# Another layout for the split keys in device memory, and shorter value visits, in a gated cross-attention block with experts

## The reference, cut to what matters

```
q, k, v = LN(x) @ W_Q, ctx @ W_K, ctx @ W_V       # 16 heads of 8 columns
score = where(mask == 0, -1e9, q k^T / sqrt(8))   # [4, 16, 256, 1601]
attn  = softmax(score) @ v
x  = x + tanh(g_xattn) * (attn @ W_T)
h  = LN(x);  probs = softmax(h @ router_w.T);  top 2 of 8 experts
x  = x + tanh(g_ffn) * sum_e combine_e * ((silu(h w1a_e) * (h w1b_e)) @ w2_e)
```

## Time and profile before

| | |
|---|---|
| Median of 3 runs (lowest to highest) | 483.82 us (476.94 to 484.28) |
| The profiled execution's own time | 477.56 us |
| Its span, first to last instruction | 475.8 us |
| Busy: PE, DVE, ACT, POOL | 93%, 74%, 57%, 18% |
| Mean granted TensorE clock | 0.975 of full speed |
| The chain that ended last: PE, DVE, ACT, DMA | 72%, 13%, 5%, 3% |
| First scores on PE | at 43.7 us |
| DMA traffic | 35.2 MB, mean 74 GB/s |

### The profile page before, as it was taken

The page is one execution under the profiler, slowest core; times in us unless marked ns, Lnnn a source line. Parts: engine busy times, 40 slices in busy tenths (PEclk is TensorE's granted clock), DMA queues, the critical chain, the costliest instruction groups (busy, mean ns, idle before and its releaser), DMA issues.

```text
span 475.8 us, 10097 instructions
## 1 busy us (share of the span) xinstructions
PE 442.1 (93%) x3864; PEld 268.5 (56%) x3866; DVE 350.7 (74%) x768; ACT 273.4 (57%) x569; POOL 86.2 (18%) x207
## 2 busy tenths in 40 slices
PE   7883999998999999999999999999999999999596
PEld 3331455654555556666655566666645476766495
DVE  3971787675668898887888987888879888542386
ACT  4201566674768666665667665665667666677131
POOL 4800507337820100000001000000001000000000
PEclk9986999999999999999999999999999999999599
DMA  7377537593735040404014403012061200000000
GB/s 272 96 162 170 124 106 160 160 269 107 187 114 104 2 91 0 92 3 91 3 28 87 94 0 80 13 43 51 2 114 43 50 2 1 2 2 24 0 1 11
DMA packets 20701, 35.23 MB, mean 74 GB/s; under 512 B 2236, under 2 KB 12924, under 8 KB 20524
## 3 DMA queue, kind: packets, MB, share of 16 engines
q1 hardware_dynamic: 19348, 33.96, 29.8%
q10 hardware_dynamic: 1304, 0.59, 0.5%
HBM read 26.49 MB, written 7.80 MB: 72 GB/s over the span
## 4 chain that ended last, share of the span: by engine, by line
PE 72%; DVE 13%; ACT 5%; issue 4%; DMA 3%; POOL 2%; POOLq 0%; SPq 0%; DVEq 0%; ACTq 0%
PE banks L1049 20%; PE banks L1015 17%; PE banks L997 13%; PE banks L1073 10%; PE banks L1081 5%; DVE chunk_max L751 4%; DVE chunk_max L733 3%; ACT probs L626 3%; PE banks L904 2%; PE banks L898 2%; DMA queries<-neg_rows 2%; DVE late L835 1%; DMA probs<-x 1%; PE banks L1131 1%; DVE late L839 1%
## 5 line engine op out<-in xcount | busy, mean ns | idle before, releaser
L751 DVE TENSOR_REDUCE chunk_max<-banks 128x1 f32<-128x512 f32 (+1 forms) x390 | 240.0, 663 | 63.4 <-PE banks L997 62.6
L626 ACT ACTIVATE probs<-banks 128x512 f32<-128x512 f32 x384 | 210.7, 603 | 88.9 <-PE banks L1015 88.3
L1015 PE MATMUL banks<-queries,keys 75*128 75x256 bf16 (+1 forms) x832 | 156.9, 275 | 10.2 <-DMA queries<-neg_rows 7.2
L997 PE MATMUL banks<-keys,queries 72*128 72x512 bf16 x480 | 146.0, 338 | 2.0 <-ACT probs L626 0.7
L1015 PEld LDWEIGHTS banks<-queries,keys 75*128 75x128 bf16 (+1 forms) x832 | 72.6, 100 | 77.6 <-DVE chunk_max L751 26.7
L1049 PE MATMUL banks<-probs,value_t 128*9 128x256 f32 x1536 | 91.9, 380 | 0.0
L1073 PE MATMUL banks<-late,w 128*128 128x256 f32 x256 | 67.2, 392 | 0.0
L1049 PEld LDWEIGHTS banks<-probs,value_t 128*9 128x9 f32 x1536 | 37.4, 90 | 43.7 <-issue 10.3
L997 PEld LDWEIGHTS banks<-keys,queries 72*128 72x128 bf16 x480 | 42.3, 97 | 21.6 <-ACT probs L626 7.6
L1073 PEld LDWEIGHTS banks<-late,w 128*128 128x128 f32 x256 | 47.9, 196 | 8.3 <-issue 2.6
L649 ACT ACTIVATE late<-banks 128x256 f32<-128x256 f32 x64 | 24.6, 385 | 45.7 <-PE banks L1073 38.8
(11 more groups left out here) (116 smaller groups left out, 261.9 us busy)
## 6 DMA issues: line engine op xcount, KB each, us to landing
keys<-k_parts SPq DMA_DIRECT2D x48, 300.2 KB
k_parts<-split SPq DMA_DIRECT2D x6, 400.2 KB, 7.6
ctx_in<-ctxT SPq DMA_DIRECT2D x3, 800.5 KB, 5.6
k_parts<-late SPq DMA_DIRECT2D x6, 400.2 KB, 4.9
queries<-q_parts SPq DMA_DIRECT2D x16, 144.0 KB
w<-w1T SPq DMA_DIRECT2D x1, 2048.0 KB, 12.7
q_parts<-q_split SPq DMA_DIRECT2D x9, 192.0 KB, 2.6
w<-mask SPq DMA_DIRECT2D x2, 800.5 KB, 7.0
```

Of the source, the lines that this page charges most:

```text
L626: nc.scalar.activation(probs[:, s % (HELD * QH), :], ring[ring_bank["scores", n]][:, :], ACT.Exp, scale=SCALE).then_inc(probs_ready, 1)
L751: nc.vector.reduce_max(dst, src, axis=AX.X).then_inc(chunk_used, 1)
L997: last = nc.tensor.matmul(dst[:, i * CW[c]:(i + 1) * CW[c]], queries[q][0:ROWS, j, t * P:(t + 1) * P], keys[q][0:ROWS, j, c * BANK:c * BAN ...
L1015: last = nc.tensor.matmul(dst, keys[q][0:KR, j, t * P:t * P + w], queries[q][0:KR, j, :], start=True, stop=not with_mask)
```

## The change

- `k_parts` becomes [batch, part, q, column, head of the unit, 1632]: for one part, one q and one column, the four heads of a unit lie side by side, and each row is padded from 1601 to 1632 columns. `split0`, `split1` and `keys` get the same padded width.
- A key load still has three transfers to 24 partitions each, but each partition's four rows of 3202 bytes become one row of 13,056 bytes. The source is now given as part by column ([3, 8] rows), where it was one run of 24 rows by 4 heads.
- A store still has 128 source partitions, but its target is given as [4 heads, 32 rows, 1632], where it was [16 heads, 8 rows, 1601].
- GpSimd clears the padding of `split0` and `split1` once each; SP waits for the first of these before it copies the rows of ones.
- Values: in units 4, 8 and 12 the tiles come two at a time.

```diff
-        k_parts_dram = nc.dram_tensor("k_parts", [B, H, PARTS, DH, SK], BF16).ap()
+        k_parts_dram = nc.dram_tensor("k_parts", [B, PARTS, NQ, DH, QH, SKP], BF16).ap()
...
-        split0 = sb("split0", [P, PARTS, SK], BF16)
+        split0 = sb("split0", [P, PARTS, SKP], BF16)
...
-        keys = [sb(f"keys{i}", [P, QH, SK], BF16) for i in range(NQ)]
+        keys = [sb(f"keys{i}", [P, QH, SKP], BF16) for i in range(NQ)]
...
                 for c in range(PARTS):
                     rows = slice(c * PARTS * DH, (c + 1) * PARTS * DH)
-                    sp.dma_start(keys[q][rows, :, :],
-                                 k_parts_dram[b, q::NQ].rearrange("j p d k -> (p d) j k")).then_inc(ld_unit[q], 16)
+                    sp.dma_start(keys[q][rows, :, :].rearrange("r j k -> r (j k)"),
+                                 k_parts_dram[b, :, q].rearrange("p d j k -> p d (j k)")).then_inc(ld_unit[q], 16)
...
-                    sp.dma_start(k_parts_dram[b, :, p], splits[b % 2][:, p, :]).then_inc(k_stored[b % 2], 16)
+                    sp.dma_start(k_parts_dram[b, p].rearrange("q d j k -> j (q d) k"), splits[b % 2][:, p, :]
+                                 ).then_inc(k_stored[b % 2], 16)
...
-            sp.wait_ge(rows_ready, 1)
+            sp.wait_ge(rows_ready, 2)
...
+            nc.gpsimd.memset(split0[:, :, SK:SKP], 0.0).then_inc(rows_ready, 1)
...
+                        if b == 1:
+                            nc.gpsimd.memset(split1[:, :, SK:SKP], 0.0).then_inc(rows_ready, 1)
...
-def value_tiles(s):
-
-    at = [VISIT // 2 * QH * (t // VISIT + 1) + 1 for t in range(KT - 1)] + [SLOTS + 2]
-    return [(at[t] // SLOTS, t) for t in range(KT) if at[t] % SLOTS == s]
+def visit(u):
+
+    return 2 if u % NQ == 0 and u >= NQ else 4
+
+
+def value_tiles(u, s):
+
+    found = []
+    for back in (1, 0):
+        n = visit(u - back)
+        at = [n // 2 * QH * (t // n + 1) + 1 for t in range(KT - 1)] + [SLOTS + 2]
+        found = found + [(back, t) for t in range(KT) if at[t] == back * SLOTS + s]
+    return found
```

More of the change, by code:

```diff
@@ L30 @@
 SK = 1601
+SKP = 1632
 H, DH = 16, 8
@@ L57 @@
 HELD = 3
-VISIT = 4
 VW = 32
@@ L256, in block_kernel @@
         key_rest = late[:, 0:SK]
-        split1 = late[:, :].bitcast(BF16)[:, 0:PARTS * SK].rearrange("p (c k) -> p c k", c=PARTS)
+        split1 = late[:, :].bitcast(BF16)[:, 0:PARTS * SKP].rearrange("p (c k) -> p c k", c=PARTS)
         splits = [split0, split1]
@@ L364, in _ @@
             sp.dma_start(gates[:, 1:2], g_f.rearrange("(o g) -> o g", o=1).broadcast_to([P, 1])).then_inc(ld_gates, 16)
-            sp.wait_ge(rows_ready, 1)
+            sp.wait_ge(rows_ready, 2)
             for i in range(NQ):
-                sp.dma_start(keys[i][NEG:KR, :, :], ones_row[:, None, :].broadcast_to([PARTS, QH, SK])
+                sp.dma_start(keys[i][NEG:KR, :, 0:SK], ones_row[:, None, :].broadcast_to([PARTS, QH, SK])
                              ).then_inc(ones_rows, 16)
@@ L370, in _ @@
                 sp.wait_ge(made, CH)
-                sp.dma_start(k_parts_dram[0, :, p], split0[:, p, :]).then_inc(k_stored[0], 16)
+                sp.dma_start(k_parts_dram[0, p].rearrange("q d j k -> j (q d) k"), split0[:, p, :]
+                             ).then_inc(k_stored[0], 16)
             sp.wait_ge(k_stored[0], 16 * PARTS)
@@ L1123, in units @@
                                     piece(piece_at(SLOTS * u + s))
-                            for back, kt in value_tiles(s):
+                            for back, kt in value_tiles(u, s):
                                 if before if back else attn:
```

## The result

The changed kernel takes **554.85 us** (median of 4 runs, 551.03 to 558.28), the kernel before, run beside it, 481.88 (4 runs, 476.94 to 484.28). The ratio is 1.1546 [1.146, 1.1632]: slower, as the likeliest case said, but 36 us over its 519 and above the range, which ended at 532. The profiled execution took 551.03 us, its span is 549.2 against 475.8, so 73.4 us have to be found.

What follows compares the result with a forecast made beforehand. PE was taken to set the pace in most units, with key loads on the path at the start. Sum: 477.6 + 16.5 + 4 + 15.5 + 9 - 3 = 519.6, rounded down to 519 us; range over all cases 472 to 532.

Steps and rivals of the forecast that it cites:

- the likeliest case: Whole kernel: fewer engines make loads and stores slower, 519 us, own range 500 to 532, chance 0.58.
- 3 and 4 engines: DMA transfers: a key load runs on 3 engines (12 before), a store on 4 (16 before).
- Both rivals that counted the SBUF side: Loads and stores: 12 and 16 engines stay; 475 us at unchanged rate (chance 0.17), 469 with faster rows (chance 0.10).
- the one by which only the start pays (491): Few engines, but slack in units 1 to 12 hides all except the start: 491 us, chance 0.10.
- 12.4 us for a unit's keys: Key loads: a unit's keys on three engines at 25.2 GB/s each take 12.4 us, 5.7 before.
- The rival with 12.9 an engine: All loads and stores: few engines that stay at 12.9 GB/s each, about 600 us, chance 0.05.
- Start, +16.5: Before the first scores: a longer last store and two slower key loads, nothing covering them, +16.5 us.
- the store gets 3.1 us longer: At the start: the last store of item 0 takes 3.1 us longer, ahead of the first key load.
- Units 1 and 2, +4.0: Unit 3's first chunk waits 2.4 us for keys; unit 2's neg rows come 4.0 late, including those 2.4.
- Unit 4, +15.5: Unit 4's neg rows wait behind loads and stores, +10.5 us, then unit 6's keys come late, +5.0.
- Units 8 and 12: Key loads issued late there, after the last expert, exceed PE's slack: +5.0 and +3.8 us, +9 together.
- Visits, -3: Units 4, 8 and 12: halved visits cut DVE's waits for PE, 1 us a unit, -3 us in all.

Runs made afterwards that it cites:

- experiment 3: The change with scratch dimensions reordered so key loads lead with 24 on both sides, each store cut in four: 501.66 us, ratio 1.0316.
- experiment 7: The changed kernel with matmuls of no use filling PE's waits, 82 of them before the first scores: 539.51 us, ratio 1.1166.
- experiment 2: The kernel before with only the visits of two tiles in units 4, 8 and 12: 485.41 us, ratio 1.0087.
- experiment 10: The kernel before with each part stored three times, so a unit's keys load as one transfer of 72 rows: 490.59 us, ratio 1.0223.
- experiment 4: The changed kernel with each store cut in four transfers of 32 partitions that lead with 32 on both sides: 524.72 us, ratio 1.0879.

## Why the prediction was wrong in size and right in kind

The step that failed most is the clock behind the waits: the prediction put it at nothing in its sum, and the runs show some 21 us of it. Next come the waits, 7 us too short in all, and the visits, whose 3 us are not there. Term by term:

- **3 and 4 engines: right.** Share 0.19 and three small packets a key transfer, share 0.26 for the stores, and experiment 3 undoes it by the order of dimensions alone. Both rivals that counted the SBUF side fell with that, and the one by which only the start pays (491) with the waits at units 2 and 4.
- **12.4 us for a unit's keys: right.** 26.5 GB/s an engine instead of 25.2. In unit 8 the queries' transfer, issued last at 309.28, lands 13.4 us later. The rival with 12.9 an engine fell.
- **Start, +16.5: short by 2.2** (18.7 for the first scores). From the issue of the load to the first scores it is 29.0 us instead of 16.1, +12.9 against 13.4 predicted. The step that failed is "the store gets 3.1 us longer": the load is issued at 33.38 instead of 27.59, +5.8. I priced the last store as if its engines were free, but the packets of the three stores (median 128 ns, mean 162) run from 13 to 32.8 us with no gap over 0.6 us: the three queue on the same four engines, and ACT's stores of the queries run in the same stretch.
- **Units 1 and 2, +4.0 for the chunk and the scores together: short by 3.4 there, and the next term missed.** The chunk waits 1.96 (2.4 predicted), the scores 5.40 (1.6). The first chunk of unit 4, inside unit 2, waits another 5.13 that stood in no term: its load is issued late, since SP waits for the stores of item 1.
- **Unit 4, +15.5: 13.35, of another make.** The neg rows wait 13.35 instead of 10.5. The 5.0 for the keys of unit 6 is zero: they are issued from 202.58, their queries last at 204.84, and land 13.4 later at 218.2; but PE, at half clock until 216.3, asks for them only at 219.56, 16.9 us behind its first scores of unit 4 (9.8 before). Experiment 7 takes half of this low clock away and the wait appears, 1.80. One loss had covered the other.
- **Units 8 and 12: near,** 3.61 and 3.75 against 5.0 and 3.8.
- **Visits, -3: wrong,** nothing on the kernel before (experiment 2). I took DVE's waits for time that could be won; the unit behind gave it back.
- **The clock: the term that was not there, 21 us.** The prediction had it only as a reason for a wider range. The kernel before showed the price: after a wait of 8 us PE ran at 0.50 until 49.7, in the earlier trace rows as 0.71 us for a pair of scores against 0.39 in the earlier trace rows. I read the row and did not multiply it by the six waits to come.

In sum: waits 52 instead of 45, visits 0 instead of -3, clock 21 instead of 0. That is 31 us, what lies between the sum, 519.6, and the profiled execution, 551.03; the median, 554.85, is above it, as the prediction allowed for. The clock's part is tested by experiment 7 for 15 us of the 21; for the rest there are only PE's busy time and the remainder.

## What to carry to other kernels

When a scratch array is regrouped to make rows longer, look first at what the outermost size of each transfer becomes on both sides: 24 against 3 cost more than any row length could give, and moving one dimension inward (experiment 3) undid most of it. Price a new wait of PE as the wait plus half of the time that it then runs at half clock; that time can only be bounded beforehand, 3 to 17 us behind a wait here, and 5.7 or 17.3 behind the same one. Where PE must wait at the start, give it something to do at once, not after the clock is down.

## What the hardware showed that was not expected

- **An engine's rate in a transfer depends on its company.** Rows of 13,056 bytes take 492 ns on three engines, 944 on twelve and 1471 on eight with 8 rows a transfer. What holds the key loads on twelve engines to 161 to 172 GB/s stays open: neither the row's length (experiment 3) nor 72 instead of 24 rows (experiment 10) moved it much by itself, and both at once were not tried.
- **An issue by SP took longer where much was queued.** Three neg transfers took 1.9 us to issue before. At the start a single one took 7 us (the chain above), the issue of `wt` 22 us (10.8 before; still 21.6 in experiment 4, whose stores are on 16 engines), and the six stores of items 2 and 3 together 21 us. SP in order of time (start, us), around the largest wait:

```profile
159.50 2.21 SPq L336 DMA_DIRECT2D keys<-k_parts  x3
161.77 0.44 SPq L341 DMA_DIRECT2D queries<-q_parts  x1
162.26 9.69 SPq L361 DMA_DIRECT2D k_parts<-split  x3
172.91 11.68 SPq L361 DMA_DIRECT2D k_parts<-late  x3
184.64 5.66 SPq L354 DMA_DIRECT2D queries<-neg_rows  x3
```

  The three neg transfers of the last row are issued over 5.7 us and the wait behind them ends at 202.68, 43 us after the keys ahead of them were issued; I had added up 40.
